# Another order of the pieces in a transformer tower written out slot by slot, on five engines

## The reference

```python
for i in range(DEPTH):                                   # 4 layers, 64 images, 197 tokens, 8 heads of 16
    y = layernorm(h, ln1_w[i], ln1_b[i])
    qkv = (y @ qkv_w[i] + qkv_b[i]).reshape(B, NTOK, 3, HEADS, hd)
    ...
    attn = jax.nn.softmax(jnp.einsum('bhnd,bhmd->bhnm', q, k) * scale, axis=-1)
    o = jnp.einsum('bhnm,bhmd->bhnd', attn, v)
    ...
    h = h + (o @ proj_w[i] + proj_b[i])
    y = layernorm(h, ln2_w[i], ln2_b[i])
    y = jax.nn.gelu(y @ fc1_w[i] + fc1_b[i], approximate=False)
    h = h + (y @ fc2_w[i] + fc2_b[i])
```

## Time and profile before

| | |
|---|---|
| median of three runs | 8434.81 us |
| the profiled execution, its own time | 8431.05 us |
| its span | 8426.6 us |
| PE busy over the span | 6782.0 us (80%) |
| DVE busy | 6795.1 us (81%) |
| ACT, POOL busy | 3191.5 us (38%), 1868.7 us (22%) |
| mean granted clock of PE | 0.879 |

### The profile page before, as it was taken

The page is one execution under the profiler, slowest core; times in us unless marked ns, Lnnn a source line. Parts: engine busy times, 40 slices in busy tenths (PEclk is TensorE's granted clock), DMA queues, the critical chain, the costliest instruction groups (busy, mean ns, idle before and its releaser), DMA issues. The chain is left out here.

```text
span 8426.6 us, 214041 instructions
## 1 busy us (share of the span) xinstructions
PE 6782.0 (80%) x81626; PEld 5204.1 (62%) x81626; DVE 6795.1 (81%) x24876; ACT 3191.5 (38%) x6847; POOL 1868.7 (22%) x2305
## 2 busy tenths in 40 slices
PE   8788888888888888835777777768888888888888
PEld 8566666666666666624555555547677677766776
DVE  2666666666666666668999999969999999999998
ACT  0444444444444444424555555522222222222221
POOL 0222222222222222223444444410000000000000
PEclk9899888888888888867888888879999999999998
DMA  6333333333333333300000000010000000000000
GB/s 195 53 47 47 47 50 48 48 48 52 48 46 45 48 47 44 48 13 5 5 4 4 5 4 4 5 33 9 10 10 8 10 10 10 8 10 10 10 8 8
DMA packets 335682, 245.80 MB, mean 29 GB/s; under 512 B 36150, under 2 KB 333401, under 8 KB 334332
## 3 DMA queue, kind: packets, MB, share of 16 engines
q1 hardware_dynamic: 334716, 232.82, 16.4%
HBM read 61.50 MB, written 13.04 MB: 9 GB/s over the span
## 5 line engine op out<-in xcount | busy, mean ns | idle before, releaser
L585 DVE TENSOR_REDUCE negmax<-S 99x4 f32<-99x788 f32 x1024 | 1001.3, 978 | 1038.0 <-PE S L352 1025.4
L471 ACT ACTIVATE probs<-ST 99x792 f32<-99x792 f32 x1024 | 851.2, 831 | 1652.3 <-PE ST L362 1651.2
L1388 PE MATMUL f_IN<-f_zT,f_wd 128*128 128x256 f32 x3200 | 880.5, 429 | 0.0
L1388 PEld LDWEIGHTS f_IN<-f_zT,f_wd 128*128 128x128 f32 x3200 | 644.4, 213 | 173.7 <-issue 50.1
L1411 PE MATMUL f_OT<-f_wu,f_act 128*128 128x128 f32 x6400 | 739.3, 277 | 1.4 <-issue 1.4
L1411 PEld LDWEIGHTS f_OT<-f_wu,f_act 128*128 128x128 f32 x6400 | 730.4, 193 | 8.3 <-issue 2.1
L1400 PE MATMUL f_AA<-f_hotp,f_hot 64*128 64x32 bf16 x38400 | 546.1, 174 | 233.1 <-DVE f_act L1656 198.2
L362 PE MATMUL ST<-qs,ks 99*99 99x198 bf16 x4096 | 580.5, 269 | 176.7 <-ACT probs L471 158.4
L352 PE MATMUL S<-ks,qs 96*99 96x198 bf16 x4096 | 578.8, 267 | 177.6 <-DVE negmax L585 150.5
L1462 ACT ACTIVATE f_act<-f_IN 128x512 f32<-128x512 f32 x800 | 478.1, 598 | 637.1 <-PE f_IN L1388 637.1
L1400 PEld LDWEIGHTS f_AA<-f_hotp,f_hot 64*128 64x128 bf16 x38400 | 511.6, 94 | 335.7 <-issue 311.6
(11 more groups left out here) (183 smaller groups left out, 13561.3 us busy)
## 6 DMA issues: line engine op xcount, KB each, us to landing
qs<-parts SPq DMA_DIRECT2D x768, 99.0 KB, 3.6
ks<-parts SPq DMA_DIRECT2D x768, 99.0 KB, 4.5
xbuf<-x_in SPq DMA_DIRECT2D x64, 588.0 KB, 4.4
f_hx<-tokens SPq DMA_DIRECT2D x50, 128.0 KB, 2.2
f_hr<-tokens SPq DMA_DIRECT2D x50, 128.0 KB, 2.1
out<-f_hr SPq DMA_DIRECT2D x50, 128.0 KB, 1.8
qs<-mrows SPq DMA_DIRECT2D x256, 9.3 KB
tokens<-h SPq DMA_DIRECT2D x64, 49.5 KB
```

What stands on the lines that cost most here:

```text
L471: A.activation(probs[:, p].rearrange("p h k w -> p h (k w)"), ST[:, :, 0:2 * W], ACT.Exp, scale=float(HD) ** -0.5).then_inc(st_taken, 1)
L585: V.tensor_reduce(negmax[:, j, :, 2 * p:2 * p + 2].rearrange("p q h -> p h q"), S[:, :, 0:2 * W].rearrange("p h (q k) -> p h q k", q=2)[:, ...
L1388: mm = nc.tensor.matmul(IN[k % 2][:, m * STEP:m * STEP + STEP], wd[:, 2 * k + m, :], zT[:, par, :], start=True, stop=True)
```

## The change

It replaces the four tables. PE gets two: pieces of `PE_FIRST` stand between the slot's `scores` and `scores_transposed`, those of `PE_AT` after both and after `attend`, as before. DVE waits for the deviations at both halves of a norm and for the added bias at both halves of an addition to h, where it waited at half 0 alone. The instructions of a group are the same in kind and number.

```diff
+PE_FIRST = {
+    0: [("turn", -1, 2), ("f2", -2, 1), ("ln1", 1, 0)],
...
+    6: [("proj", -1, 0), ("k", 1, 1), ("proj", -1, 1), ("max", 0, 2)],
...
+    15: [("f1", -1, 1), ("f1", -1, 2)],
+}
...
-            12: [("oraw", 0, 2), ("f1", -1, 0), ("f1", -1, 1), ("f1", -1, 2), ("f1", -1, 3)],
+    14: [("f1", -1, 0), ("f1", -1, 1), ("f1", -1, 2), ("f1", -1, 3)],
...
+    9: [("stats1", 2, 0), ("stats1", 2, 1), ("stats2", -1, 1)],
...
             def normalise(n, norm, a):
-                if a == 0:
-                    upto(dve, rstd_done[norm], n + 1)
+                upto(dve, rstd_done[norm], n + 1)
...
             def add_to_h(name, n, norm, a):
-                if a == 0:
-                    upto(dve, bias_added[norm], n + 1)
+                upto(dve, bias_added[norm], n + 1)
...
+                if 0 <= ahead[0] < NT:
+                    scores(*ahead, p)
+                pieces(first)
+                if 0 <= n < NT:
+                    scores_transposed(n, j, p)
+                if p == 0 and 0 <= behind[0] < NT:
+                    attend(*behind, 1)
+                if p == 2 and 0 <= n < NT:
+                    attend(n, j, 0)
+                pieces(then)
```

More of the change, by code:

```diff
@@ L57, in start @@
     Count.made.clear()
+PE_FIRST = {
+    0: [("turn", -1, 2), ("f2", -2, 1), ("ln1", 1, 0)],
+    2: [("k", 1, 0)],
+    3: [("oT", -1, 0), ("turn", -1, 3), ("v", 1, 0)],
+    5: [("oT", -1, 1)],
+    6: [("proj", -1, 0), ("k", 1, 1), ("proj", -1, 1), ("max", 0, 2)],
+    7: [("turn", 0, 0)],
+    9: [("v", 1, 1)],
+    10: [("max", 0, 3), ("turn", 0, 1)],
+    13: [("max", 1, 0)],
+    15: [("f1", -1, 1), ("f1", -1, 2)],
+}
+PE_AT = {
+    0: [("f2", -2, 0), ("max", 0, 1)],
+    1: [("q", 1, 0), ("ln1", 1, 1)],
+    3: [("q", 1, 1)],
+    12: [("ln2", -1, 0)],
+    13: [("ln2", -1, 1), ("f1", -1, 0)],
+    15: [("f1", -1, 3)],
+}
+ACT_AT = {
+    1: [("max", 0, 1), ("oraw", -1, 3), ("high", 1, 0), ("high", 1, 1), ("ln1", 1, 1)],
+    2: [("oT", -1, 0)],
+    3: [("high", 1, 2)],
+    4: [("oT", -1, 1)],
+    5: [("oraw", 0, 0), ("high", 1, 3), ("max", 0, 2)],
+    7: [("oraw", 0, 1)],
+    9: [("max", 0, 3)],
+    12: [("ln2", -1, 0), ("oraw", 0, 2)],
+    13: [("ln2", -1, 1), ("max", 1, 0)],
+    14: [("f1", -1, 0), ("f1", -1, 1), ("f1", -1, 2), ("f1", -1, 3)],
+    15: [("ln1", 2, 0)],
+}
+DVE_AT = {
+    0: [("norm1", 1, 1), ("f2", -2, 0)],
+    2: [("split", 1, 0), ("split", 1, 1)],
+    3: [("o", -1, 3)],
+    4: [("v", 1, 0)],
+    5: [("split", 1, 2), ("proj", -1, 0)],
+    6: [("split", 1, 3)],
+    7: [("o", 0, 0), ("stats2", -1, 0)],
+    8: [("proj", -1, 1)],
+    9: [("stats1", 2, 0), ("stats1", 2, 1), ("stats2", -1, 1)],
+    10: [("o", 0, 1)],
+    11: [("v", 1, 1), ("norm2", -1, 0)],
+    12: [("norm2", -1, 1)],
+    15: [("norm1", 2, 0), ("o", 0, 2), ("f2", -1, 1)],
+}
+POOL_AT = {
+    4: [("max", 0, 3), ("rstd2", -1, 0), ("max", 1, 0)],
+    5: [("rstd1", 2, 0)],
+    11: [("add", -1, 1)],
+    13: [("max", 1, 1)],
+    14: [("max", 1, 2)],
+    15: [("add", 2, 0)],
+}
 def build_tower(nc, ctx, B, DEPTH, x_in, base_in, convw_in, layer_in, h, ident):
@@ L149, in build_tower @@
         WK = [bank(f"WK{i}") for i in range(3)]
[L156 to L184, removed]
-            12: [("oraw", 0, 2), ("f1", -1, 0), ("f1", -1, 1), ("f1", -1, 2), ("f1", -1, 3)],
-            13: [("max", 1, 0)],
-        }
@@ L188, in build_tower @@
[L188 to L213, removed]
         def walk(table):
@@ L218, in walk @@
                 for s in range(SLOTS):
-                    yield n, s, [(what, n + d, a) for what, d, a in table.get(s, []) if 0 <= n + d < NT]
+                    yield n, s, [(what, n + d, a) for what, d, a in table.get(s, ()) if 0 <= n + d < NT]
         place = {}
[L222 to L225, removed]
+        for (n, s, first), (_, _, then) in zip(walk(PE_FIRST), walk(PE_AT)):
+            for piece in first + then:
+                place[piece] = (len(place) % 3, len(place) // 3)
         bank_ready = [sem(f"bank_ready{b}") for b in range(3)]
@@ L295, in stack_max @@
                 sp.dma_start(qs[STACK:STACK + PARTS, n % 2, :, j, :], mrows[:, j, :]).then_inc(max_stacked[j], 16)
-            load_weights(0)
-            load_weights(1)
+            for layer in range(min(2, DEPTH)):
+                load_weights(layer)
             for n in range(-1, NT):
@@ L423, in back, with pieces @@
                 mm.then_inc(is_ready("f2", n, a), 1)
[L425 to L437, removed]
+            def pieces(of):
+                for what, m, a in of:
                     if what in ("ln1", "ln2"):
@@ L458, in _ @@
                         back(m, a)
+            pe.wait_ge(filled, 6)
+            for (n, s, first), (_, _, then) in zip(walk(PE_FIRST), walk(PE_AT)):
+                j, p = divmod(s, 4)
+                ahead, behind = divmod(number(n, j) + 2, G), divmod(number(n, j) - 1, G)
+                if 0 <= ahead[0] < NT:
[8 more added lines that the diff above has]
+                pieces(then)
         @block.scalar
```

## The result

The changed kernel takes 7965.72 us (median of four runs, 7946.25 to 7981.6) against 8439.31 us, the median of four of the kernel before: a ratio of 0.9439, 95% interval 0.9411 to 0.9467. That is 474 us or 5.6% faster; 8025 was predicted, within 7860 to 8250. The profiled execution took 7981.6 us.

The account below looks back on a forecast made before the run. PE was taken as the engine with most work, not full: 54.05 us a group = 39.05 work + 11.6 waits + 3.4 slow clock. With 39.05 + 6.0 + 2.6 = 47.65 over 64 groups, 410 us go: 8021, stated as 8025, range 7860 to 8250.

Parts of the forecast that it names:

- the clock: Whole group: PE's loss to the throttled clock falls from 3.4 to 2.6 us, following the waits.
- Gelu: Slots 15 and 0: PE's 2.55 us wait for the exp behind gelus and table loads goes; 0.05 comes.
- walked: Timed by stepping through one group from scores of slot 15, at fixed prices from the before kernel's timelines.
- Banks: Slots 1 to 7: 3.2 us of waits for banks held by DVE's split go; 0.95 us come.
- DMA: Slots 8 and 9: scores of slot 8 waits 1.5 us for the first stack; v waits 0.1 in slot 9.
- The upper bound of 1.3 us more: Slot 8: extra wait if the stack takes 9.05 us to issue, not 7.7; the shorter was taken.
- DVE: Mainly slots 10 to 13: statistics delay DVE's maximum, scores of slot 11 waits 2.05 us; v and norm2 wait 0.85 and 0.5.
- The sum of the waits: Whole group: new waits of 6.0 us from start to start against 11.6 before, so -5.6 us.
- DMA and clock: Rival: both stacks issue in 9.05 us and the clock gains nothing, 50.75 us a group, 8220 us; chance 0.24.
- Clock stays full: Rival: with waits of 6.0 us the slow clock disappears, 45.05 us a group, 7855 us; chance 0.10.
- SP's queue as the bound: Rival: SP's chain of stacks and small DMAs reaches 54.05 us at 10.7 us issue; 8594 us at 12; chance 0.07.
- The drain of the table load, 8197: Slot 0: with drains of 1380 ns at ACT's table switches, PE would stand 2.75 us, giving 8197 us.

Follow-up runs that it names:

- e2: Changed kernel with the pieces between scores and scores_transposed in slots 15 and 0 put back behind scores_transposed and attend; 8277 us.
- e4: Changed kernel with three unused filler matmuls a group in PE's wait for the stack's DMAs before scores of slot 8; 8053 us.
- e6: Changed kernel with SP stacking part by part as each part is ready, instead of all twelve DMAs behind the last split; 7932 us.
- e12: Changed kernel with e6's stacking, the fourth max DMA between the second stack's parts, and stats1 of both halves in slots 13 and 14; 7597 us.
- e10: e6 plus two unused filler matmuls a group before scores_transposed of slot 11, where PE waits for DVE's maximum; 7764 us.

## Why the prediction was right

The direction and the mechanism of the waits held; one term, the clock, was mis-sized by a factor of three. The total came close in part by luck: the waits gave back 0.7 us a group less than forecast and the clock 1.8 more.

- *Gelu.* Predicted: 2.55 us go, 0.05 come. The list has no wait for ACT left, and f2 (2010.04) and ln1 stand over the table load (2009.91) and the exp behind it, as walked. e2 shows that the place between the two halves of the slot does it.
- *Banks.* Predicted: 3.2 us go, 0.95 come, 0.55 of it at scores of slot 6. The waits for the splits are gone, and of the new ones slot 6 alone shows, with 0.39. Right, and a little too careful.
- *DMA.* Predicted 1.5 us at slot 8, measured 2.8 a group, 3.25 in the group shown. PE came 1 us sooner than walked, and from the first issue of the stack to scores it took 13.3 us (2021.94 to 2035.23), not 12.0. The upper bound of 1.3 us more, which I set aside, has the right size by chance: it came from a slower issue, and the issue took the 7.7 us walked (2021.94 to 2029.61). Between its end and scores lie 5.6 us, and 5.1 to 5.7 in the next three groups, where 4.3 were walked.
- *DVE.* Predicted 4.05 us from start to start, in slots 5, 6 and 11 to 13, some 3.3 as idle time; measured 2.4. The row of statistics is there, but scores of slot 11 waits 1.2 us on average and not 2.05: PE came late to it from the slow stretch. In e4 and e6, where slots 9 and 10 ran at full clock, the same wait is 1.8.
- *The sum of the waits.* Idle time was to fall by 5.6 less the 0.6 for four fewer broken overlaps, 5.0; it fell by 4.3. The long wait at slot 8 is what is missing.
- *The clock*, the step that failed in size. Predicted -0.8 us, of a cost of 3.4 before and 2.6 after; measured is some -2.6 us, with 5.9 before and 3.3 after. The kernel e12 ran at full clock in this stretch, with 941.48 / 24.8 = 38.0 us busy a group for the same matmuls. So the kernel before lost 44.5 - 38.0 = 6.5 us to it, less some 0.6 for more broken overlaps, and the changed one 41.2 - 38.0, 3.3 before rounding. A second way agrees: each matmul that ran wholly at half clock, priced by its distance to the next against its kind at full clock, gives 5.9 and 3.4 us a group (an estimate from all PE records of both traces, 1500 to 2500 us). The cost before was misread because the length of a record was used. Of scores, a record grows from 249 to 376 ns at half clock, but the distance from one to the next from 85 to 166. In the group shown, a record of four goes from 0.55 (2006.33) to 0.88 (2036.86), and the step to the next piece from 0.38 to 0.68. So 267 over 248 ns is far less than what PE loses. Scores also stand at half clock less often than the rest (14% of them, at a slow share of 26% in this stretch), while f2 was at 335 ns before and 277 after. The half of the throttled time that the Trainium skill gives (TensorE: Matmul & The Clock Gate, Terms), and that I set aside for the row, is nearer: by the clock of this stretch it would be 7.0 us before and 3.7 after, against 5.9 and 3.3.
- *The rivals.* DMA and clock: did not come. Both stacks did not take 9.05 us, scores_transposed of slot 12 does not wait for its small DMA, and the clock went the other way; only the wait at slot 8 was longer than walked. Clock stays full: no, 0.92. SP's queue as the bound: the stacks of the group shown took 7.7 and 8.4 us to issue, below the 10.7. The drain of the table load, 8197: no sign of it, the exp starts 0.02 us behind the load (2009.91 + 1.28 to 2011.21).

Together: 54.05 - 4.3 - 3.3 = 46.5 us. Over 64 groups that would be 483 us, and the profiled executions differ by 449: between 1500 and 2500 us the kernel before is slower than its mean from 400 to 3640 us, which is 968 maxima in 3240 us or 53.55 us a group.

What stays open is what exactly makes the clock fall. e4 and e10 both fill a wait of PE; one loses 87 us, the other gains 168. In e4 the slow stretch left slots 8 and 9 and grew in slots 11 to 14, behind the next waits; in e10, where the wait just before it was filled, it nearly went (20% of a group to 3%). No run here gives a rule for where it goes.

## What to carry to other kernels

In a hand-written order, look at pieces that stand behind two halves that each need another engine's answer: put between them, a piece gives that engine its length of time to catch up. Here this was worth 311 us at the gelu and 298 in the other slots. Where the clock of TensorE falls with its waits, price it from the distance between starts at both clocks, for all forms of matmul and weighted by where they stand, and not from the length of one form's records. Then go on removing waits: the last 2.9 us of idle time between the changed kernel and e12 brought 6.2 us a group.

## What the hardware showed that was not expected

Adding work made a kernel faster: two matmuls of 516 ns on average, each recorded twice, put into a wait of 1.8 us took 168 us off 7932. The same idea three slots earlier, in a longer wait of 2.8 us and on the changed kernel, cost 87 us. And of the 2.8 us a group of waiting that e6 removed, 2.1 came back: 1.1 as waits for DVE and 1.0 as busy time at a lower clock.
